# Exponentials of the second scores in two ScalarE operations a step instead of four

## What is computed

```
scale = 1 / sqrt(8)
for layer in 0, 1, 2:                       # plain attention over the text tokens
    q, k, v = heads(x @ Wq), heads(ctx @ Wk), heads(ctx @ Wv)
    x = merge(softmax(q @ k^T * scale) @ v) @ Wo + b + x
layer 3:                                    # text attention, and beside it an image branch
    probs_t = softmax(q @ k_text^T * scale) # 73 tokens
    qsem    = l2norm(probs_t @ ctx_text)    # per head
    fused   = q @ k_ip^T * scale + 0.5 * (qsem @ l2norm(ctx_ip)^T)
    x = merge(probs_t @ v_text + softmax(fused) * mask @ v_ip) @ Wo + b + x
```

## Time and profile before

| | us |
|---|---|
| median of 3 runs | 2264.23 (2263.96 to 2268.26) |
| the profiled execution | 2264.95 |
| its span, first to last instruction | 2263.2 |
| TensorE busy with matmuls | 2086.4 (92%) |
| VectorE busy | 1481.7 (65%) |
| ScalarE busy | 1075.1 (48%) |
| GpSimd busy | 458.7 (20%) |
| the exponentials of line 1027, 768 operations | 372.9 |
| granted TensorE clock over the span | 0.97 of full speed |

### The profile page before, as it was taken

One profiled execution on the slowest core, in us unless ns is written; L12 is line 12 of the kernel. 1 busy time (PEld: TensorE's weight loads), 2 busy tenths in 40 slices (PEclk: granted clock), 3 DMA queues, 4 the chain that ended last, 5 costly groups with the idle time before them and its releaser, 6 DMA issues.

```text
span 2263.2 us, 75842 instructions
## 1 busy us (share of the span) xinstructions
PE 2086.4 (92%) x26394; PEld 1697.5 (75%) x26394; DVE 1481.7 (65%) x4449; ACT 1075.1 (48%) x2733; POOL 458.7 (20%) x870
## 2 busy tenths in 40 slices
PE   2699999999999999999999999999999999999975
PEld 1567877887787788778778877887887788778764
DVE  3236776777677676767767766776676677667654
ACT  0245554455445455544545554554554455555431
POOL 0112122212212221221222122122212222222110
PEclk9889999999999999999999999999999999999975
DMA  3111111211111121112111111211211121111000
GB/s 82 49 43 50 52 43 42 52 50 39 47 52 44 41 52 51 38 46 52 45 41 52 52 38 47 53 44 40 52 52 38 47 53 44 39 53 38 22 10 5
DMA packets 108576, 101.31 MB, mean 45 GB/s; under 512 B 42240, under 2 KB 84952, under 8 KB 108184
## 3 DMA queue, kind: packets, MB, share of 16 engines
q1 hardware_dynamic: 104556, 92.88, 15.1%
q10 hardware_dynamic: 3628, 3.33, 0.6%
HBM read 34.13 MB, written 5.41 MB: 17 GB/s over the span
## 4 chain that ended last, share of the span: by engine, by line
PE 78%; SPq 8%; DVE 5%; issue 4%; DMA 2%; ACT 2%; ACTq 1%; DVEq 0%; POOLq 0%; POOL 0%
PE ps_s L738 11%; PE ps_c L816 10%; PE ps_s L771 8%; PE ps_c L886 6%; PE ps_k L839 6%; PE ps_k L644 5%; PE ps_q L717 5%; PE ps_c L875 4%; PE ps_k L670 4%; PE ps_s L788 4%; PE ps_k L844 4%; SPq L584 3%; PE ps_c L891 3%; PE ps_c L852 2%; SPq L577 2%
## 5 line engine op out<-in xcount | busy, mean ns | idle before, releaser
L1131 DVE TENSOR_REDUCE top<-ps_s 128x6 f32<-128x462 f32 (+3 forms) x1024 | 511.3, 546 | 88.2 <-PE ps_s L738 84.3
L1027 ACT ACTIVATE p_t<-ps_s 116x512 f32<-116x512 f32 (+1 forms) x768 | 372.9, 545 | 48.9 <-PE ps_s L771 46.9
L738 PE MATMUL ps_s<-k_blocks,q_sb 32*128 32x231 f32 (+1 forms) x3584 | 347.8, 384 | 20.3 <-issue 18.5
L816 PE MATMUL ps_c<-p_t,v_rows 116*27 116x128 f32 (+1 forms) x7168 | 288.7, 284 | 14.8 <-DMA v_rows<-v_img 12.3
L738 PEld LDWEIGHTS ps_s<-k_blocks,q_sb 32*128 32x128 f32 x3584 | 229.9, 185 | 84.9 <-issue 31.3
L816 PEld LDWEIGHTS ps_c<-p_t,v_rows 116*27 116x27 f32 (+1 forms) x7168 | 214.1, 108 | 86.5 <-issue 49.3
L1055 ACT ACTIVATE o_t<-ps_c 128x256 f32<-128x256 f32 x256 | 98.1, 383 | 368.3 <-PE ps_c L875 302.7
L1354 POOL TENSOR_TENSOR k_blocks<-k_sb,mask_k 128x231 f32<-128x231 f32 x384 | 211.8, 573 | 267.6 <-PE ps_s L771 252.5
L771 PE MATMUL ps_s<-q_sb,k_blocks 32*116 32x128 f32 (+1 forms) x5376 | 223.8, 283 | 27.7 <-DMA q_sb<-top_t 15.0
L839 PE MATMUL ps_k<-gram,p_t 116*128 116x154 f32 x896 | 210.6, 317 | 41.6 <-DVE weighted L1171 41.6
L771 PEld LDWEIGHTS ps_s<-q_sb,k_blocks 32*116 32x116 f32 (+1 forms) x5376 | 186.3, 175 | 63.7 <-issue 52.0
(11 more groups left out here) (118 smaller groups left out, 3595.3 us busy)
## 6 DMA issues: line engine op xcount, KB each, us to landing
v_rows<-v_img SPq DMA_DIRECT2D x128, 227.4 KB
context<-in_ctx SPq DMA_DIRECT2D x64, 336.0 KB, 3.0
q_sb<-top_t SPq DMA_DIRECT2D x576, 6.0 KB
v_rows<-v_img SPq DMA_DIRECT2D x64, 115.2 KB
v_rows<-v_img SPq DMA_DIRECT2D x64, 112.2 KB
v_rep<-v_dram SPq DMA_DIRECT2D x64, 50.0 KB
q_sb<-top_t SPq DMA_DIRECT2D x192, 2.0 KB
gram<-g_img SPq DMA_DIRECT2D x64, 46.3 KB
```

Source lines behind the costliest of these rows:

```text
L738: ins = pe.matmul(ps_s[:, z * 512 + j * GT:z * 512 + j * GT + n], q_sb[c % 3][lo:lo + QUAD, j * S:(j + 1) * S], k_blocks[c % 3][lo:lo + QU ...
L816: ins = pe.matmul(ps_c[t % 2][32 * (g % 4):32 * (g % 4) + UC, g // 4 * S:(g // 4 + 1) * S], v_rows[b % NC][0:n, v:v + UC], p_t[c % 3][0:n, ...
L1027: act.activation(to, source, ACT.Exp, scale=SCALE).then_inc(p_ready, 1)
L1131: dve.tensor_reduce(top[c % 2][:, z * BH:z * BH + m], s.rearrange("p (h t) -> p h t", t=T)[:, :, 0:n], AX.X, ALU.max).then_inc(s_top, 1)
```

## The change

`exps` of the first three layers takes bank 3 as before, and then banks 0, 1 and 2 in one operation of 1536 columns, which waits until all four banks are written and raises `p_ready` by three. The third and fourth call do nothing. The copies of the last layer stay four operations. Nothing else is edited.

```diff
             def exps(k, c, i):
 
+
                 z = BANKS[i]
-                act.wait_ge(e_psum, raised(k, exists, c - 1, per=4, more=i + 1))
+                whole = not ip(c) and i == 1
+                if not ip(c) and i > 1:
+                    return
+                act.wait_ge(e_psum, raised(k, exists, c - 1, per=4, more=4 if whole else i + 1))
                 if i == 0:
                     act.wait_ge(u_psum, raised(k, exists, c - 3))
                     if ip(c - 3):
                         act.wait_ge(w_psum, raised(k, ip, c - 3, per=4))
-                n = groups_in(z) * 2 * S
+                n = (3 if whole else 1) * groups_in(z) * 2 * S
                 to, source = p_t[c % 3][0:FIRST, z * 512:z * 512 + n], ps_s[0:FIRST, z * 512:z * 512 + n]
                 if ip(c):
                     act.activation(to, source, ACT.Copy).then_inc(p_ready, 1)
                 else:
-                    act.activation(to, source, ACT.Exp, scale=SCALE).then_inc(p_ready, 1)
+                    act.activation(to, source, ACT.Exp, scale=SCALE).then_inc(p_ready, 3 if whole else 1)
```

## The result

| | before | changed |
|---|---|---|
| median of 4 runs | 2266.24 (2263.96 to 2270.93) | 2297.70 (2294.91 to 2302.95) |
| span of the profiled execution | 2263.2 | 2297.2 |
| TensorE busy with matmuls | 2086.4 (92%) | 2020.2 (88%) |
| ScalarE busy | 1075.1 (48%) | 1052.9 (46%) |
| six cycles in the middle of the run | 197.8 | 201.3 |

The ratio is 1.0142, with a 95% interval of 1.0121 to 1.0162: slower by 31.5 us, beside the 33 that were forecast.

The account below looks back on a forecast made before the run. TensorE, busy 92%, was taken to bound the kernel, so ScalarE's savings count only where TensorE waits. 2264.95 + 38.0 (image step) - 5.0 (layer-2 step) = 2297.95, forecast 2297 us, range 2277 to 2315.

Parts of the forecast that it names:

- The mechanism: Image step: f_exp behind the wide operation ends 0.95 us later, f_sum 0.87, line 860's turn 0.77 to 0.87, 0.80 taken.
- The price of the wide operation: ScalarE: 1536 columns take 1.475 us by the slope over columns, beside 1.57 for three operations of 512.
- The burst of the image step: TensorE's scores in the image step: over 0.17 us earlier, a gain lost in the later wait for o_last.
- the first rival: f_sum's wait: the late f_exp doesn't reach TensorE, both bursts gain, 15.2 us faster, 2249; chance 0.07.
- the layer-2 step: Scores behind the layer-2 exponentials: 0.08 us gained a step, over some 62 steps 5.0 us faster.
- The wait for the maxima's DMA: TensorE's wait in the image step's successor swallows about 1.0 us of a body's six delays.
- The sum: Whole run: 2264.95 + 38.0 - 5.0 = 2297.95 us, forecast as 2297; chance 0.82.
- the end of the run: Last cycles: no exponentials ahead of f_exp, so only 60 steps, ten bodies, were counted as slower.
- the terms named for the lower end: Range: start and turn's release 5 us either way, another 1.0 a body swallowed takes 10; given as 2278.
- the second: TensorE's other waits in a body: they swallow 4.3 of the 4.8 us of delay, giving 2265; chance 0.05.
- The third: Wide operation pays for each bank, 1.80 us; image and layer-2 steps both lose, giving 2335; chance 0.06.
- the two rules weighed: ScalarE: breaking up instructions (the change costs time) against fixed cost (it gains); first for image step, second for layer-2 step.

Follow-up runs that it names:

- fexp_behind_four: Kernel before with its four operations, only f_exp moved behind the fourth, no wide operation; 2297.18 us, ratio 1.0158 to before.
- image_step_only: Changed kernel with the wide operation in the image step alone, layers 1 and 2 keeping four operations; 2300.68 us, ratio 1.0165 to before.
- results_ahead_of_fsum: Changed kernel with `results` of pair t-2 moved ahead of f_sum, f_rec and p_ip on VectorE; 2255.70 us, ratio 0.9957 to before.
- image_step_four: Changed kernel with four operations back in the image step, the wide one kept in layers 1 and 2; 2258.79 us, ratio 0.9977 to before.
- four_release: Changed kernel, four operations in the image step, TensorE's score banks in the order 3, 0, 1, 2; 2248.36 us, ratio 0.9939 to before.
- four_results_release: Changed kernel, four operations in the image step, `results` ahead of f_sum on VectorE, TensorE's banks as 3, 0, 1, 2; 2243.26 us, ratio 0.9915.

## Why the prediction was right, and where it was off

- **The mechanism held, link by link.** f_exp was to be 0.95 late against the first exponential. It ends 1013.85 - 1011.71 = 2.14 behind that start, where it was 931.37 - 930.23 = 1.14: 1.00. f_sum follows 0.10 behind f_exp, as in the earlier trace rows, and o_last comes 0.14 before the turn, as in the earlier trace rows. The turn was to be 0.77 to 0.87 later, 0.80 taken; the rows give 0.82, and so do the medians over the loop (3.049 and 3.871 us).
- **The price of the wide operation** was 1.475, and is 1.450. The Trainium skill ("ScalarE: Activation LUTs", section "What ACT_TABLE_LOAD costs") comes to 1.466 by its 186 ns and 0.833 ns a column; the trace agrees within 0.016, a little better than with my slope. It begins 0.145 later than bank 0's operation did, not 0.08; both errors together leave f_exp 0.05 later than predicted.
- **The burst of the image step** was to be over 0.17 earlier. The exponentials do end 0.13 earlier (1.886 us behind the last second scores, 2.018 before), because f_exp is out of the middle: fexp_behind_four has 1.866. But the burst starts 0.145 behind the wide operation, at 2.031, and needs another 0.989, so it would be over at 3.020, 0.03 before the old turn at 3.049. This is lost in the wait for o_last, as predicted of the larger number. Had the first rival come true, it would have gained 0.03 a step and not 0.17.
- **The term that failed is the layer-2 step**: "0.01 is lost, 0.08 gained", 5.0 us over the run. The loop's medians show 0.016, 1.0 us. I took the release behind the wide operation to be as quick as behind bank 2's (1018.51 to 1018.56). But that one released a product with one wait, and the wide operation releases the burst's first, with two: 0.14 instead of 0.05. The exponentials' own end came 0.12 earlier, a little more than the 0.09 expected. The Trainium skill's 93 ns of overlap (the same page and section) would have made this step gain 0.18. The trace doesn't agree: the exponentials end 0.12 earlier, and the operation of 1024 columns saves 0.05 over two.
- **The wait for the maxima's DMA** was to swallow 1.0 of a body's delays. In the body before it was 1.1, in the one after there is none, and over the run it falls from 15.0 us to 6.6.
- **The sum.** A body was to grow by 3.8 - 0.5 = 3.3 us; it grows by 3.5. By these terms it is 6 x 0.82 = 4.9, less 1.1 for the DMA and 0.1 for the layer-2 step, 3.7. Over ten bodies 38.2 - 1.0, where 38.0 - 5.0 stood. What kept the total near the forecast is the end of the run, which I counted at nothing: from the sixtieth start of line 860 to its last, the sixty-fourth, it is 102.5 us instead of 105.3. So 34.4, beside a span that is 34.0 longer. Two errors of 4 and 3 us had opposite signs, and that was luck: the end was shorter by the clock granted there (0.77 instead of 0.51 in the last cycle but one, which took 22.6 us instead of 26.4), and image_step_only, with the same image step, has 105.3 again. In the range, the terms named for the lower end give 2282 and not 2278; the result lies well above either.
- **The rivals.** The first (the delay doesn't reach TensorE) falls with the 63 waits at line 860, the second (other waits take it back) with the body's 3.5 us. The third, each bank paid in full at 1.80, falls with 1.450. The mechanism of the first is real, though: results_ahead_of_fsum is that case, made by an edit to VectorE's queue.
- Of the two rules weighed, that of "Perfetto Trace Analysis" in the Trainium skill, section "Optimizing Scalar/DVE Operations" ("breaking up instructions may allow work to be completed sooner") is what the runs show in the image step.

**Where the other 4 us come from, and what stays open.** image_step_four is 0.23% faster than the kernel before, and the change 0.23% faster than image_step_only (there the intervals overlap): 5 us each, just what I had predicted for the layer-2 step. Yet the layer-2 step accounts for 1 us of it. In the profiled executions most of the rest is the clock. One cycle of each body holds the loop's jump back, and it comes in two lengths. Two of image_step_four, as above from one start of line 860 to the next:

```profile
1159.66:1193.39 33.73, 30.82 (x412) 25.40 (x412) 22.70 (x69) 16.27 (x38) 7.02 (x13) 1.00 0.16 46
1356.04:1391.35 35.31, 32.30 (x412) 26.56 (x412) 23.15 (x69) 16.34 (x38) 7.02 (x13) 0.95 0.16 44
```

Of its eight such cycles, three have a clock of 1.00 and take 33.7 to 33.8 us, five have 0.95 and take 34.9 to 35.5. The kernel before has 0.95 in all eight (35.0 to 35.5). Three fewer at some 1.5 us are 4.4, of the 5.1 by which the first and the sixtieth start of line 860 lie closer together. In the changed kernel seven of eight have the low clock and in image_step_only eight; their bodies differ by 0.1, and the 2.8 by which their ends differ are in the last cycle but one, 22.6 us at 0.77 and 25.4 at 0.55. The median of a body with two lengths also misleads: four_release's is 1.6 us shorter than image_step_four's, but the mean over eight bodies is 0.8 shorter, of which the layer-2 step's 0.07 explains 0.4 and the clock 0.3 (three cycles with the low clock instead of five).

Two things stay open. No run kept the clock fixed, so how much of the 5 us in the medians over many executions is clock isn't known. And why the low clock gets rarer isn't shown. The kernels without a wide operation in layers 1 and 2 have it in 7 or 8 of 8 bodies, those with one in 5 to 8, and those with the new order of the banks besides in 3 or 4.

## What to carry to other kernels

Before merging operations on an engine with time to spare, look at what stands behind them in its queue, and at what stands behind *that* operation's consumer in the next queue: 0.09 us saved put a 0.26 us operation 1.0 us later, and 31 us came of it. An operation that needs nothing of the late one should stand ahead of it, which here took the loss back. (The further 0.4% at the end of the run came with a higher granted clock, so it is no promise for another kernel.) Before a gain of a few tenths of a per cent is put down to an edit, compare the granted clock of the stretch in which it appears. And where one wide operation releases several buffers at once, let the consumer begin with a piece that waits for nothing else.

## What the runs showed of the hardware

- One operation over three PSUM banks takes 1450 ns, near the 1475 of the slope over columns. Three operations of one bank in a row take 1.57 us, since their records overlap; so the wide one ends 0.12 earlier where it can start at the same time (layer-2 step). Where it has to wait for the last bank (image step) it starts 0.145 later and saves nothing: 1.98 us with the bank of 256 columns ahead, beside 1.96 for four operations.
- The product that waits for two semaphores starts some 0.14 us behind the end of its producer, one that waits for a single one 0.05. In the queue the second wait stands as an instruction of its own, of 51 ns. Of the weight loads alone it is 0.11 and 0.05.
- With the granted clock near 0.5, the same 28 weight loads and their matmuls at the end of the run keep TensorE busy for 7.6 us, and for 4.4 at 0.79.
- TensorE's clock falls to half (1.2 of 2.4 GHz) for a while in most bodies, right behind the loop's jump back, where its weight loads stand idle for 2.9 us and its matmuls for 2.5. Such a stretch makes the cycle some 1.5 us longer. In the kernel before, first the load behind that pause, then the stretch behind it and a later one:

```profile
984.27 0.81 PEld L738 LDWEIGHTS ps_s<-k_blocks,q_sb 32*128 32x128 f32 x13 [2.90 <-issue]
```

```profile
985.00:988.50 3.50, 3.50 (x42) 2.92 (x37) 2.77 (x6) 0.77 (x2) 0.00 (x0) 0.54 0.04 9
996.00:999.60 3.60, 3.60 (x56) 3.23 (x52) 2.73 (x8) 1.71 (x6) 0.54 (x2) 1.00 0.44 125
```

The granted clock is 0.54 in the first and 1.00 in the second, with TensorE busy throughout both. The eight bodies have 8 such stretches before, 7 after the change, 5 in image_step_four and 3 in four_results_release.
